# Two more rows of the stacked queries carry the row maxima of a windowed attention

## The reference

```python
for i in range(0, S, w2):                       # w2 = 32, w4 = 16
    start = max(0, i - w4)
    end = min(S, i + window_size - w4)
    attn = softmax(einsum('bqd,bkd->bqk', q[:, start:end] * scale, k[:, start:end]))
    wo = einsum('bqk,bkd->bqd', attn, v[:, start:end])
    # the overlap with the window before is blended with a ramp
```

## Time and profile before

| | us |
|---|---|
| median of 3 runs | 371.27 |
| lowest and highest run | 369.61 and 377.07 |
| span of the profiled execution, first to last instruction | 361.3 |
| outside of the span, median of the runs less the span | 10.0 |

### The profile page before, as it was taken

How to read it: one execution, slowest core, us unless ns; L and a number is a source line. 1 busy time by engine, 2 the same in 40 slices (tenths; PEclk the granted TensorE clock), 3 DMA queues, 4 the chain that set the end, 5 groups by cost and what they waited for, 6 DMA issues and landing times.

```text
span 361.3 us, 10050 instructions
## 1 busy us (share of the span) xinstructions
PE 305.9 (85%) x3668; PEld 231.7 (64%) x3668; DVE 244.1 (68%) x709; ACT 152.3 (42%) x298; POOL 78.6 (22%) x115
## 2 busy tenths in 40 slices
PE   2256697999898998997898979888787989989993
PEld 1123554777676876876657757556576878868892
DVE  2454605837849759488456584858887899698986
ACT  2135073337346174463551635465455313824220
POOL 4443101302304104032020011030553012202020
PEclk9766588569789699799886999999999999999998
DMA  6009386270360903505308100000000000100000
GB/s 188 24 2 201 95 175 164 79 127 4 105 98 2 185 12 98 100 6 144 60 3 181 23 5 2 2 2 2 0 2 0 2 1 0 31 0 23 8 29 29
DMA packets 38540, 20.01 MB, mean 55 GB/s; under 512 B 5604, under 2 KB 38120, under 8 KB 38504
## 3 DMA queue, kind: packets, MB, share of 16 engines
q1 hardware_dynamic: 38504, 19.53, 24.7%
HBM read 11.13 MB, written 8.13 MB: 53 GB/s over the span
## 4 chain that ended last, share of the span: by engine, by line
PE 47%; DVE 22%; issue 9%; SPq 9%; DMA 7%; ACT 4%; POOL 1%; DVEq 0%; ACTq 0%; POOLq 0%
PE bank L637 5%; PE bank L422 5%; PE bank L386 5%; PE bank L432 4%; PE bank L403 4%; DVE xh L1007 3%; PE bank L398 3%; SPq L293 3%; SPq L320 3%; DMA kst<-stack_scratch 3%; PE bank L442 3%; PE bank L619 3%; DVE acc L1342 3%; PE bank L620 2%; PE bank L621 2%
## 5 line engine op out<-in xcount | busy, mean ns | idle before, releaser
L1048 DVE TENSOR_REDUCE nm<-bank 128x8 f32<-128x512 f32 x64 | 43.3, 690 | 29.0 <-PE bank L386 28.3
L857 POOL TENSOR_TENSOR rs<-ve,mhalf 128x2 f32<-128x2 f32 (+1 forms) x24 | 19.8, 827 | 141.5 <-DVE ve L1004 134.7
L720 ACT ACTIVATE prob<-bank 128x512 f32<-128x512 f32 x64 | 37.8, 601 | 11.8 <-PE bank L403 10.0
L422 PE MATMUL bank<-prob,vb 128*64 128x128 f32 x512 | 40.7, 305 | 2.1 <-issue 1.6
L386 PE MATMUL bank<-kst,qst 48*64 48x64 bf16 x1024 | 31.0, 208 | 7.7 <-DMA kst<-stack_scratch 4.3
L809 ACT ACTIVATE sg<-bank 128x512 f32<-128x512 f32 x32 | 18.9, 600 | 43.6 <-PE bank L621 42.1
L637 PEld LDWEIGHTS bank<-wds,hh 128*128 128x128 f32 x256 | 32.3, 191 | 7.1 <-issue 5.5
L726 ACT ACTIVATE pvs<-bank 128x512 f32<-128x512 f32 x32 | 19.1, 596 | 41.9 <-PE bank L422 41.9
L386 PEld LDWEIGHTS bank<-kst,qst 48*64 48x64 bf16 x1024 | 24.4, 120 | 18.4 <-issue 18.0
L637 PE MATMUL bank<-wds,hh 128*128 128x128 f32 x256 | 33.7, 277 | 2.8 <-DVE acc L1342 2.3
L422 PEld LDWEIGHTS bank<-prob,vb 128*64 128x64 f32 x512 | 31.7, 151 | 4.4 <-issue 2.7
(11 more groups left out here) (139 smaller groups left out, 514.0 us busy)
## 6 DMA issues: line engine op xcount, KB each, us to landing
stack_scratch<-parts SPq DMA_DIRECT2D x16, 216.0 KB, 2.3
qst<-stack_scratch SPq DMA_DIRECT2D x16, 216.0 KB, 3.9
kst<-stack_scratch SPq DMA_DIRECT2D x16, 216.0 KB, 5.3
stack_scratch<-parts SPq DMA_DIRECT2D x16, 144.0 KB, 2.3
stack_scratch<-parts SPq DMA_DIRECT2D x16, 72.0 KB, 2.0
mrow<-mt SPq DMA_DIRECT2D x64, 4.0 KB, 1.7
out_x<-fin SPq DMA_DIRECT2D x4, 256.0 KB, 2.3
xs<-in_x SPq DMA_DIRECT2D x1, 896.0 KB, 6.7
```

The costliest lines, as they stand in the source:

```text
L422: m = pe.matmul(psv[WIN * (h2 % 2):WIN * (h2 % 2) + WIN, P * (h2 // 2):P * (h2 // 2) + P], vb[n][:, eo, H2 * par + h2, :, :, :], prob[gp % ...
L720: act.activation(prob[g // 2 % 2][:, :, g % 2, :], psb[g % 2][:].rearrange("p (h q) -> p h q", h=H2), ACT.Exp).then_inc(exp_done, 1)
L1048: dve.tensor_reduce(nm[:, g, :], psa[g % 2][:].rearrange("p (h k) -> p h k", h=H2), AX_X, ALU.max, negate=True).then_inc(max_done, 1)
```

## The change

The keys' stack gets two rows of ones behind the 48 (partitions 48, 49 and 112, 113), written once at the start by four DVE memsets over partitions 32 to 63 and 96 to 127 (the reads then overwrite 32 to 47 and 96 to 111). The queries' stack gets the high and the low part of minus the maxima in its rows 48 and 49, and `scores_b` multiplies over 50 rows. The matmul L398, `mrow`, `monesb` and their input are gone. Since a token stands in an even and in an odd window, with another maximum in each, there are two query stacks of 256 columns for each buffer, one for even and one for odd windows: `read_stacks` has six DMAs a batch, two of them for the second copy of the queries (512 bytes in a piece where the queries had 576), and `scores_a` waits for all six. `write_mrow` still has four DMAs, each from 16 partitions of `mt` into one row of the stack; `cut_m` writes its parts in another order. `read_stacks(0)` also waits for the memsets, and `scores_b` separates its waits with a semaphore instruction (`apart`).

```diff
             def read_stacks(b, n):
                 sp.wait_ge(b_done, after(b_done, 8 * (b - 1)))
                 apart(sp)
-                for k, (stack, written) in enumerate(((qst[n], q_written), (kst[n], k_written))):
+                for k, stack, written, cols in ((0, qst[n][0], q_written, slice(0, S)),
+                                                (1, kst[n], k_written, slice(0, LINE)),
+                                                (0, qst[n][1], q_written, slice(LINE - S, LINE))):
                     sp.wait_ge(written, after(written, 48 * (b + 1)))
                     apart(sp)
                     for r in range(2):
-                        src = scr_rows[ds(b, 1), r, k].rearrange("b r h n -> (b r) h n")
+                        src = scr_rows[ds(b, 1), r, k, :, :, cols].rearrange("b r h n -> (b r) h n")
                         sp.dma_start(stack[64 * r:64 * r + ROWS], src).then_inc(stack_ready, 16)

             def write_mrow(b, n, hf):
                 sp.wait_ge(mt_ready, after(mt_ready, 2 * b + hf + 1))
                 apart(sp)
-                for part in range(2):
-                    for half in range(2):
-                        r = 2 * part + half
-                        sp.dma_start(mrow[n][r:r + 1, 32 * hf:32 * hf + 32, :],
-                                     mt[32 * part:32 * part + 32, WIN * half:WIN * half + WIN]
-                                     ).then_inc(mrow_ready, 16)
+                for par in range(2):
+                    for part in range(2):
+                        r, at = 64 * par + ROWS + part, 32 * part + 16 * par
+                        sp.dma_start(qst[n][hf][r:r + 1].rearrange("o h (s q) -> o (h s) q", s=2),
+                                     mt[at:at + 16, :]).then_inc(mrow_ready, 16)
...
             write_parts(0)
+            sp.wait_ge(ones_ready, after(ones_ready, 4))
             read_stacks(0, 0)
...
-                pe.wait_ge(stack_ready, after(stack_ready, 64 * (b + 1)))
+                pe.wait_ge(stack_ready, after(stack_ready, 96 * (b + 1)))
...
-                pe.matmul(bank[:], monesb[:], mrow[n][:, H2 * g:H2 * g + H2, :], start=True, stop=False,
-                          skip_group_check=True)
-                rows_ = slice(64 * par, 64 * par + ROWS)
+                rows_ = slice(64 * par, 64 * par + MROWS)
                 for h2 in range(H2):
                     for half, at in halves:
                         m = pe.matmul(bank[WIN * half:WIN * half + WIN, WIN * h2:WIN * h2 + WIN],
-                                      kst[n][rows_, h2, at:at + WIN], qst[n][rows_, h2, at:at + WIN],
-                                      start=False, stop=True, skip_group_check=True)
+                                      kst[n][rows_, h2, at:at + WIN], qst[n][eo][rows_, h2, at - 32 * eo:at - 32 * eo + WIN],
+                                      start=True, stop=True)
...
-                src = nm[:, 4 * hf:4 * hf + 4, :].rearrange("p g h -> p (g h)")
-                pool.tensor_copy(mp[:, 0, :], src).then_inc(mp_step, 1)
+                src = nm[:, 4 * hf:4 * hf + 4, :].rearrange("p (a s) h -> p a h s", a=2)
+                high, low = [mp[:, part, :].rearrange("p (a h s) -> p a h s", a=2, s=2) for part in range(2)]
+                pool.tensor_copy(high, src).then_inc(mp_step, 1)
...
+            for n in range(2):
+                for par in range(2):
+                    dve.memset(kst[n][64 * par + 32:64 * par + 64].bitcast(F32), TWO_ONES).then_inc(ones_ready, 1)
...
-            dve.tensor_copy(monesb[:], monesf[:]).then_inc(consts, 1)
```

More of the change, by code:

```diff
@@ L17 @@
+import struct
 from contextlib import ExitStack
@@ L39 @@
 ROWS = HD * TERMS
+MROWS = ROWS + 2
 VC = 2 * HD
@@ L55 @@
 ZONE_HIGH = 0.5
+TWO_ONES = struct.unpack("f", struct.pack("I", 0x3F803F80))[0]
 def build(nc, x, wqkvp, w1, w2, wg, wu, wd, wr, temp, c_t, wmod, cols, rows, ident, alpha, vmask,
-          mones, earlier, out):
+          earlier, out):
     ctx = ExitStack()
@@ L130, in build @@
         parts = sb("parts", [P, 3, 2, LINE], BF16)
-        qst = [sb(f"qst{i}", [P, H2, LINE], BF16) for i in range(2)]
-        kst = [sb(f"kst{i}", [P, H2, LINE], BF16) for i in range(2)]
         nm = sb("nm", [P, 8, H2])
@@ L158, in build @@
         with ExitStack() as attention:
-            mrow = [attention.enter_context(nc.sbuf_tensor(f"mrow{i}", [4, 8 * H2, WIN], BF16)) for i in range(2)]
             vb = [attention.enter_context(nc.sbuf_tensor(f"vb{i}", [P, 2, NH, 2, 2, VC], F32)) for i in range(2)]
+            qst = [[attention.enter_context(nc.sbuf_tensor(f"qst{i}{eo}", [P, H2, S], BF16)) for eo in range(2)]
+                   for i in range(2)]
+            kst = [attention.enter_context(nc.sbuf_tensor(f"kst{i}", [P, H2, LINE], BF16)) for i in range(2)]
         wpart = sb("wpart", [P, 2, E, P], F32R)
@@ L179, in build @@
         consts_pool = sem("consts_pool")
+        ones_ready = sem("ones_ready")
         sc_step, sc_exp = sem("sc_step"), sem("sc_exp")
@@ L305, in _ @@
             sp.dma_start(wa[:], wqkvp.rearrange("p (c d) -> p c d", c=4)).then_inc(wa_loaded, 16)
-            for dst, src in ((alph, alpha), (vmsk, vmask), (monesf, mones)):
+            for dst, src in ((alph, alpha), (vmsk, vmask)):
                 sp.dma_start(dst[:], src).then_inc(small_loaded, 16)
             write_parts(0)
+            sp.wait_ge(ones_ready, after(ones_ready, 4))
             read_stacks(0, 0)
@@ L382, in scores_a @@
                 par, halves = spans(g)
+                eo = g // 4
                 rows_ = slice(64 * par, 64 * par + ROWS)
@@ L386, in scores_a @@
                         m = pe.matmul(psa[g % 2][WIN * half:WIN * half + WIN, WIN * h2:WIN * h2 + WIN],
-                                      qst[n][rows_, h2, at:at + WIN], kst[n][rows_, h2, at:at + WIN],
+                                      qst[n][eo][rows_, h2, at - 32 * eo:at - 32 * eo + WIN], kst[n][rows_, h2, at:at + WIN],
                                       start=True, stop=True)
@@ L395, in scores_b @@
                     pe.wait_ge(exp_done, after(exp_done, 8 * b + g - 1))
+                apart(pe)
                 par, halves = spans(g)
-                bank = psb[g % 2]
-                pe.matmul(bank[:], monesb[:], mrow[n][:, H2 * g:H2 * g + H2, :], start=True, stop=False,
-                          skip_group_check=True)
-                rows_ = slice(64 * par, 64 * par + ROWS)
+                bank, eo = psb[g % 2], g // 4
+                rows_ = slice(64 * par, 64 * par + MROWS)
                 for h2 in range(H2):
@@ L489, in _ @@
             modulation(2, bk[2])
-            pe.wait_ge(small_loaded, after(small_loaded, 96))
+            pe.wait_ge(small_loaded, after(small_loaded, 80))
             pe.wait_ge(wa_loaded, after(wa_loaded, 16))
-            pe.wait_ge(consts, after(consts, 3))
+            pe.wait_ge(consts, after(consts, 2))
             pe.wait_ge(modt_ready, after(modt_ready, 2))
@@ L740, in _ @@
             copy_mod(2, bk[2])
-            act.wait_ge(small_loaded, after(small_loaded, 96))
-            act.wait_ge(consts, after(consts, 11))
+            act.wait_ge(small_loaded, after(small_loaded, 80))
+            act.wait_ge(consts, after(consts, 10))
             act.wait_ge(consts_pool, after(consts_pool, 5))
@@ L900, in cut_m @@
                 apart(pool)
[L901 to L902 removed]
+                src = nm[:, 4 * hf:4 * hf + 4, :].rearrange("p (a s) h -> p a h s", a=2)
+                high, low = [mp[:, part, :].rearrange("p (a h s) -> p a h s", a=2, s=2) for part in range(2)]
+                pool.tensor_copy(high, src).then_inc(mp_step, 1)
                 pool.wait_ge(mp_step, after(mp_step, 4 * b + 2 * hf + 1))
[L904 removed]
+                pool.tensor_tensor(low, src, high, ALU.subtract).then_inc(mp_step, 1)
             pool.memset(mhalf[:], -0.5).then_inc(consts_pool, 1)
@@ L911, in _ @@
             pool.wait_ge(consts_pool, after(consts_pool, 5))
-            pool.wait_ge(small_loaded, after(small_loaded, 96))
+            pool.wait_ge(small_loaded, after(small_loaded, 80))
             first_root_x(0)
@@ L1126, in _ @@
             ln_b(0)
-            dve.wait_ge(small_loaded, after(small_loaded, 96))
+            dve.wait_ge(small_loaded, after(small_loaded, 80))
             dve.tensor_copy(idb[:], idf[:]).then_inc(consts, 1)
-            dve.tensor_copy(monesb[:], monesf[:]).then_inc(consts, 1)
             dve.tensor_scalar(bqs[:], col[:, BQ:BQ + 1], SCALE, None, ALU.mult).then_inc(consts, 1)
@@ L1348, in _ @@
             dve.reciprocal(rtemp[:], temps[:]).then_inc(consts, 1)
-            dve.wait_ge(consts, after(consts, 12))
+            dve.wait_ge(consts, after(consts, 11))
             for g in range(NG - 2):
@@ L1442 @@
         "vmask": vmask,
-        "mones": mones.reshape(4, P),
         "earlier": np.tril(np.ones((E, E), np.float32), -1)[None],
```

5 lines of the change are left out of this document (removed).

## The result

The changed kernel takes 390.5 us (median of 4 runs, 383.9 to 394.5), the kernel before 374.2 beside it (369.6 to 378.6). Executions of one kernel differ by their granted clock, and the ratio compares the faster ones of both kernels alone, so it isn't the quotient of the medians: 1.039, with an interval from 1.026 to 1.052, slower by 3.9%. The forecast of 373 and its range up to 383 were both too low; the second rival (382) named the right side and mechanism, at too small a price.

The account below looks back on a forecast made before the run. PE was taken to bound most of each step, ACT and DVE the rest, with the stacks' DMA path 2.3 us behind. Start +3.0, steps +0.4, end -1.6: +1.8 on 371.3, so 373 us, range 360 to 383.

Parts of the forecast that it names:

- the second rival: In the steps, every wait for the second query copy brings a clock fall: 25.8 us a step, 382 us; chance 0.30.
- What bounds the kernel, and the removed matmul: Four of a step's eight removed matmuls lie on PE's path, four beside ACT and DVE: 8.4 us over five steps.
- The reads: Stack reads grow from 864 to 1200 KB a batch: +2.0 us by bytes, ends +0.5 and +2.6.
- The wait and the clock: scores_a waits about 1.1 us for DMA; a clock fall follows in half the steps: 24.1 us a step, +0.4 over five.
- The start: Up to batch 2's first scores_a, the extra copy delays reads and weights: some 3.0 us later, at 85.7.
- The end: After batch 7's first scores_a, five of twelve remaining removed matmuls stand on the chain: -1.6 us.
- The base: Profiled span of 361.3 us plus 10.0 us taken as outside it gives the median, 371.3 us.
- The first: Rival: reads cost only +0.5 us, PE stays the bound at 21.95 us a step: -11 us, 360 us; chance 0.20.
- The third: Rival: the turn_sums stall and DMA path absorb everything, batch 2 starts on time: 370 us; chance 0.50 together with the forecast.
- the signs: Expected in the profile: stack waits of 0.5 to 2 us, PE busy 20 us less, ctxn wait growing to about 2.

Follow-up runs that it names:

- e2: The kernel before without the spreading matmul, so row maxima aren't subtracted in the second scores, its DMAs of the maxima kept; 364.3 us, ratio 0.979.
- e7: The changed kernel with one query stack, four reads a batch, the odd windows' maxima overwriting the even ones'; 363.8 us, ratio 0.977.
- e6: The kernel before with each stack read cut into two DMAs of half a line, same bytes in twice the pieces; 373.8 us against 373.7.
- e5: The changed kernel with three filler fp32 matmuls ahead of the stack wait in each first scores_a but batch 0's; 379.8 us, ratio 1.021.
- e3: The changed kernel plus a matmul of the removed shape at the head of each scores_b, its result overwritten; 395.2 us, ratio 1.058.
- e9: e7 plus one filler fp32 matmul ahead of turn_sums 2 in each step that prepares a batch; 368.0 us, ratio 0.989.
- e10: e7 plus two filler fp32 matmuls ahead of turn_sums 2 in each step that prepares a batch; 365.5 us, ratio 0.985.
- e8: The kernel before, unchanged, profiled a second time in a single execution; span 371.5 us, own time 373.4 us.
- e1: The changed kernel with a separate semaphore for the second query copy, awaited only by scores_a of groups 4 to 7; 371.1 us, ratio 0.988.

## Why the prediction was wrong

**What bounds the kernel, and the removed matmul: right.** Four matmuls of a step on PE's path and four beside the ACT and DVE chain gave 8.4 us for the steps and 1.6 for the end. e2 measured 8.2 in all, with five steps that are 7.5 us shorter in its profile than in the earlier trace rows, and e7 9.9 in the medians (8.7 by the ratio).

**The reads: the right measure, too small.** Forecast +2.0 us a batch, by bytes, with ends of +0.5 and +2.6. Batch 2's set fills the engines for 8.1 us, the forecast was 7.2. From the first read's issue to the scores_a that waits for the last one the steps of the changed kernel took 9.5 to 11.7 us, in the mean 10.3; I had 9.2 (129.7 less 120.5). e6 shows that bytes were the right measure. The rule of the Trainium skill's DMA: Bandwidth & Descriptors (Specifications), by which pieces of at least 512 bytes reach line rate, isn't borne out: 156 GB/s for a set of 512 and 576 bytes.

**The wait and the clock: the step that failed.** "I expect such a fall in about half of the steps, costing 1.9 of the possible 2.7 us", +0.95 a step. The run paid from scores_a to project_qk 7.56, 7.56, 7.55, 5.95 and 7.56 us against 4.33: something in all five, and 2.9 a step in the mean. e5 takes the idle time out and leaves the wait: 4.3 in all five. The trace of before had held one wait of this kind and one fall behind it. I took a half against that, and my only reason was that each step has a stretch at half clock already and the fall may merely move. It didn't merely move: some 78 us at the lower level over the five steps, against some 34.

Added up for a step: 27.8 us measured against 24.1. Of the 3.7, 2.0 is this term, 1.1 the reads, 0.4 the writes ahead of them and 0.3 ACT's and DVE's part. The last three, 1.8 us, lie on the DMA's way alone, so they lengthened the wait itself, from the forecast 1.1 us to 2.9 in the mean (2.10 to 4.01). The prediction had said that the second rival decides "as soon as scores_a waits about as long as the 1.38 us there". So the undersized DMA terms also put the kernel where the low clock comes behind every wait. The rule of the Trainium skill's TensorE: Matmul & The Clock Gate (HAM oscillation), a fall behind each wait for a DMA, holds in each of these five steps. Behind waits of about 1 us it doesn't hold each time: the clock stayed up behind 1.04, 1.15 and 1.25 us in e3, e9 and e10, and fell behind 1.01 us in e6 (106.34, project_qk 7.15 us after it).

**The start: the right shape, too small.** Forecast 39.2 and 85.7 for batches 0 and 2; measured 38.83 and 88.28. Batch 1 was forecast at 56.7 and came at 57.31. The missing 2.6 us come behind that: SP issued batch 2's writes at 73.14, 4.9 us later than before (68.27), where the prediction's terms give 2.8 (3.4 less 0.6), and then the reads took 8.1 us and not 7.2.

**The end: can't be read.** Forecast -1.6, measured +0.6. e8 shows that this stage differs by 11 us between executions of one program, by the clock alone.

**The base: the right number for a wrong reason.** I took 10.0 us as lying outside of the span. It is 1.9, and the rest was an execution with a rare clock (0.85 in the window, 0.79 in e8). The steps that I read it by were not touched by this: five steps took 120.0 us there and 118.6 in e8 (83.07 to 201.67).

**The rivals.** The first fell with the reads' rate. The second was the answer in kind, priced at 25.8 a step and 382; the steps took 27.8 and the start +5.6 in place of +3.0. The third fell. Of the signs, the second rival's came: waits for qst<-stack_scratch in every batch, four of five steps over 25.5 us (one of 25.4), half clock behind each wait. Two others didn't: PE was busy only 3.3 us less and not 20, and its waits for ctxn before turn_sums (0.5 to 1.3 us in the steps) didn't grow to 2.

The account by the runs: the removed matmul gives 2.1% (e2), and the wait for the second copy in the first scores_a takes 5.1% (the changed kernel's 1.039 against e1's 0.988). Of this e5 assigns 1.8% to the lower clock behind the wait, measured as 1.039 against 1.021. That split is not exact, since the intervals overlap and a filler that ends late also costs; the traces agree with it, 9 us less for the five steps. The second copy's bytes may take about 1.1% (e1 against e7), which the intervals don't separate from nothing. Why the clock stays low for as long as 20 or 44 us while PE is busy isn't settled by these runs.

## What to carry to other kernels

Where a resource gets a second transfer, ask which instruction needs it first, and give it a semaphore of its own: here four of eight groups never touch the second copy, and a shared count made all wait for it. When engines hand work round a loop, price the loop and not the engine: a microsecond of DMA or of low clock inside it comes back in every turn (here 3.7 us more than forecast in each of five), while 26 us of busy PE were worth 8. For the same reason a higher clock gained nothing where PE then waited for the reads (e9, e10). And before a second copy is read, look whether the first can be overwritten in time: that version's ratio (e7, 0.977) is that of the removed matmul alone (e2, 0.979).

## What the runs showed of the hardware

- The granted clock can stay at 1.2 GHz while TensorE is hardly idle: 44 us with PE busy for 42.4 of them (e3), 23.6 with 22.8 (e8), with the small matmuls of this attention. In e8 and the first profile the same instructions ran at different levels in the same place.
- Windows filled by stack reads from DRAM onto 48 partitions at a time show 153 to 189 GB/s (153 and 172 with pieces of 288 bytes, 156 and 176 with 512 and 576 mixed, 189 with 576 and little else, of which the reads' own 864 KB make 170), while weights in pieces of 512 bytes onto all partitions ran at 251. What sets the lower rate wasn't tried.
- Useless matmuls ahead of a wait made a kernel 1.8% faster (e5), and the same kind in another wait made none faster (e9, e10).
- The clock fell in or behind all five waits of 2.10 to 4.79 us for a DMA with which the changed kernel's steps begin. Behind waits of about 1 us it went both ways: up until project_qk had ended behind 1.04 (e3), 1.15 (e9) and 1.25 us (e10), down behind 1.01 (e6).
